# A graph attention edge pass: ScalarE's exponentials before its copy of a block, TensorE's first block behind the turn of the maxima

## What is computed

```python
src, dst = (edge_index[0], edge_index[1])
xl = (x @ W_l + b_l).reshape(n, HEADS, C)
xr = (x @ W_r + b_r).reshape(n, HEADS, C)
e = (edge_attr @ W_e).reshape(-1, HEADS, C)
g = jax.nn.leaky_relu(xl[src] + xr[dst] + e, NEG_SLOPE)
logits = jnp.einsum('ehc,hc->eh', g, att)
amax = jax.ops.segment_max(logits, dst, num_segments=n)
ex = jnp.exp(logits - amax[dst])
denom = jax.ops.segment_sum(ex, dst, num_segments=n)
alpha = ex / (denom[dst] + 1e-16)
out = jax.ops.segment_sum(xl[src] * alpha[..., None], dst, num_segments=n)
```

## Time and profile before

| What | Value |
|---|---|
| median of 3 timed runs | 5762.61 us |
| range of the timed runs | 5761.96 to 5765.02 us |
| span of the profiled execution, the only time known of it | 6618.7 us |
| span over median | 856.1 us, 14.9% |
| TensorE busy | 4926.0 us (74%) |
| VectorE busy | 3854.6 us (58%) |
| ScalarE busy | 1920.7 us (29%) |
| GpSimd busy | 4014.0 us (61%) |
| mean granted TensorE clock | 0.630 of full speed |

### The profile page before, as it was taken

How to read it: one execution, slowest core, us unless ns; L and a number is a source line. 1 busy time by engine, 2 the same in 40 slices (tenths; PEclk the granted TensorE clock), 3 DMA queues, 4 the chain that set the end, 5 groups by cost and what they waited for, 6 DMA issues and landing times. The chain is left out here.

```text
span 6618.7 us, 104783 instructions
## 1 busy us (share of the span) xinstructions
PE 4926.0 (74%) x33518; PEld 3702.2 (56%) x33518; DVE 3854.6 (58%) x7688; ACT 1920.7 (29%) x4445; POOL 4014.0 (61%) x4125
## 2 busy tenths in 40 slices
PE   5566777777777776467777777777776469999689
PEld 4455666766667765356666566666655332222289
DVE  3122355555555542356666666666665469999855
ACT  1111222222222211112222222222211149999811
POOL 4555566666666665366666666666666627787634
PEclk6555566565565555555555555555555579999899
DMA  6644355555555544244444444444444334343298
GB/s 164 113 111 132 103 150 150 148 144 146 145 149 149 148 136 116 65 118 130 132 132 131 131 127 130 132 131 131 131 131 115 72 101 129 124 129 124 69 336 301
DMA packets 897045, 902.75 MB, mean 136 GB/s; under 512 B 635824, under 2 KB 779480, under 8 KB 880373
## 3 DMA queue, kind: packets, MB, share of 16 engines
q1 hardware_dynamic: 568404, 708.29, 33.9%
q0 software_dynamic: 115488, 115.45, 9.0%
q10 hardware_dynamic: 212608, 72.31, 4.8%
HBM read 656.88 MB, written 239.54 MB: 135 GB/s over the span
## 5 line engine op out<-in xcount | busy, mean ns | idle before, releaser
L507 POOL DMA_INDIRECT mlp_G<-mlp_src,src_cols x1612 | 1531.3, 950 | 1027.5 <-PE mlp_z L873 480.7
L507 POOL DMA_INDIRECT gatv_G<-gatv_src,src_cols x1612 | 1529.2, 949 | 940.1 <-DMA X<-in_x 435.7
L691 DVE TENSOR_TENSOR mlp_hots<-mlp_in_psum,src_lo 128x1024 bf16<-128x1024 bf16 x608 | 416.6, 685 | 734.3 <-remote 573.7
L909 PE MATMUL gatv_sums<-gatv_msg,gatv_same 128*128 128x68 f32 x3234 | 712.0, 390 | 151.7 <-issue 149.8
L909 PEld LDWEIGHTS gatv_sums<-gatv_msg,gatv_same 128*128 128x128 f32 x3234 | 688.2, 310 | 171.2 <-issue 169.1
L909 PE MATMUL mlp_sums<-mlp_zs,mlp_same 128*128 128x64 f32 x3234 | 676.5, 389 | 64.8 <-issue 64.6
L909 PEld LDWEIGHTS mlp_sums<-mlp_zs,mlp_same 128*128 128x128 f32 x3234 | 648.4, 301 | 66.0 <-issue 65.9
L2201 POOL TENSOR_TENSOR keys<-src_lo,gsoft_ring 128x512 f32<-128x512 f32 (+1 forms) x448 | 505.1, 1133 | 182.5 <-ACT src_lo L2344 172.7
L2266 PE MATMUL gsoft_acc<-keys,masks 128*64 128x512 f32 (+1 forms) x1568 | 558.2, 621 | 77.0 <-DVE keys L2440 42.1
L869 PE MATMUL gatv_z<-attr_w,gatv_attrT 112*128 112x448 f32 x462 | 422.3, 1017 | 206.3 <-DVE gatv_msg L597 107.9
L873 PE MATMUL mlp_z<-mlp_win,mlp_hot 128*128 128x64 bf16 x4851 | 384.6, 232 | 240.2 <-issue 236.2
(11 more groups left out here) (481 smaller groups left out, 8498.5 us busy)
## 6 DMA issues: line engine op xcount, KB each, us to landing
mean_block<-blocks SPq DMA_DIRECT2D x62, 1568.0 KB
gsoft_ring<-blocks SPq DMA_DIRECT2D x105, 896.0 KB
sums_gatv<-gatv_out_rows SPq DMA_DIRECT2D x231, 252.0 KB
mlp_rel<-rel_rows SPq DMA_DIRECT2D x116, 448.0 KB
gatv_rel<-rel_rows SPq DMA_DIRECT2D x116, 448.0 KB
sums_mlp<-mlp_out_rows SPq DMA_DIRECT2D x231, 224.0 KB
blocks<-masks SPq DMA_DIRECT2D x31, 1568.0 KB
blocks<-work SPq DMA_DIRECT2D x31, 1568.0 KB
```

The lines of the kernel that those rows point to most:

```text
L507: pool.indirect_dma_start(out=G[:, b.gq, j * L.gathered:(j + 1) * L.gathered], out_offset=None, in_=L.gather_table, in_offset=bass.Indirec ...
L691: last = nc.vector.tensor_tensor(hot_of[:, slot(b, k), :, :, :], bc(steps2_of[:, 0:w, :], 1, [P, OCTET // K2, w, K2]), bc(of_step[:, cols] ...
L909: last = pe.matmul(sums[b.q % 2][:, j * L.msg:(j + 1) * L.msg], same[:, b.q, j, :], rhs, start=True, stop=True)
```

## The change

In the second pass ScalarE's copy of block 1 of batch d moves from ahead of `exponentiate(d)` to behind `nonlinear(i)`. TensorE's block 0 of batch p moves from ahead of `make_z(i+1)` to between `turn_max(p)` and `turn_logits(i)`. The first pass keeps its order. No instruction is added or removed, and no wait condition is changed.

```diff
@@ ScalarE, step(i) @@
                 p, d = i + (-1), i + (-2)
-                if d.exists() and builds(d):
+                if not soft and d.exists() and builds(d):
                     copy_octet(d, per_batch - 1)
                 if soft and d.exists():
                     exponentiate(d)
                 if L.window and i.exists():
                     nonlinear(i)
+                if soft and d.exists() and builds(d):
+                    copy_octet(d, per_batch - 1)
                 if p.exists() and builds(p):
                     copy_octet(p, 0)
@@ TensorE, step(i) @@
                 p = i + (-1)
-                if p.exists() and builds(p):
+                if not soft and p.exists() and builds(p):
                     build_octet(p, 0)
                 if L.window and (i + 1).exists():
                     make_z(i + 1)
@@
                 if soft and p.exists():
                     turn_max(p)
+                    if builds(p):
+                        build_octet(p, 0)
                 if soft and i.exists():
                     turn_logits(i)
```

## The result

The kernel after the change takes **5720.11 us** (median of 4, 5718.07 to 5721.94); the kernel before took 5763.82 us beside it (4 runs, 5761.96 to 5771.25). The ratio is 0.9918, 95% interval 0.9904 to 0.9932: faster by 0.8%, 44 us. The forecast was 5655 us, a gain of 108. Direction and range held. The gain forecast was two and a half times too large.

The account below looks back on a forecast made before the run. The ring was taken to bound batches with blocks: 9.31 - 1.69 + 0.81 = 8.43 us, below GpSimd's 8.75, so 0.56 us times 192 is 108 us gained. 5762.6 - 108 = 5655 us, range 5585 to 5780.

Parts of the forecast that it names:

- The floor: GpSimd's gathers, second pass: seven a batch cost 8.75 us, the next bound once the ring is shorter.
- The ring's 9.31 us: Batches with blocks: cycle of last block, copy, exponentials, weighing, `gatv_z`, turns, sums; 9.31 us, taken as the bound.
- ScalarE's 1.69 us out of the ring: Copy, exponentials, weighing and handover leave the cycle, covered by TensorE's sums and last block: 1.69 us less a batch.
- The sign that I gave for it: In the changed kernel's profile, exponentials (L774) start within 0.3 us of L590's end; before, 2.5 us.
- The first block's 0.81 in the chain: TensorE's first block, formerly built during a wait, now stands between two turns and adds 0.81 us a batch.
- The upper bound of the gain: TensorE's own work as floor, if GpSimd is shorter in timed runs: 0.88 us a batch, 169 us.
- The 0.73 us from the block's recorded end to its copy: TensorE to ScalarE: by the skill's rule 0.73 us belongs to the ring, making the gain 1.29 us a batch, 248 us.
- Rival 1: GpSimd's gather train binds the timed runs too: 0 to 25 us gained, 5738 to 5763; chance 0.20.
- Rival 2: VectorE's weighing is held by adding the gathered rows, not by ScalarE: no gain, 5763 us; chance 0.11.
- Rival 3: Slower: behind late gathers TensorE's first block adds 0.81 us a batch, 39 to 156 us in all; chance 0.14.
- Rival 4: More than forecast: the ring loses 0.73 us too, or TensorE's clock rises: up to 357 us, 5406; chance 0.08.

Follow-up runs that it names:

- ScalarE's part alone: Kernel before with only ScalarE's copy of block 1 moved behind the ReLU, TensorE's order as before: 5804.42 us, ratio 1.0061.
- the pair that lifts the floor: Kernel before and kernel after, each with one gather in seven left out in the second pass from its ninth batch: 5703.59 and 5539.98 us.
- before again: Kernel before, unchanged, profiled a second time: 5749.23 us, span 5747.5 us, 9.00 us a batch with blocks.

## Why the prediction was right in direction and wrong in size

**The floor: right.** GpSimd's "8.75, which becomes the next bound" measured 8.77, and the kernel after, 180 us faster with six gathers, shows it to be that bound.

**The ring's 9.31 us: the step that failed.** The mechanism held, but this term of "9.31 - 8.75 = 0.56 us a batch" was sized too large. In the ordinary execution a batch takes 9.00, not 9.31, so the gain is 0.23 us and not 0.56; times 192 that is 44 us for 108. Of the 0.31 us, 0.21 are the turn at 1.2 GHz itself (9.10 in the timeline above): it is the sums, 3.14 reckoned and 2.89 measured. The 3.14 was read in a long execution, where the sums stood still once and were longer than the 0.33 us of that accounts for; what stretched them is open. The other 0.10 are what two things leave together, neither of which the sum had: 44 of 166 batches are at 2.4 GHz and take 8.12 us, and the 122 others take 9.33 on average, some of them behind late gathers. That the balance is as small as 0.10 is chance, and the executions' own spread is as large. The granted clock of the stretch is 0.59, in the execution that was read 0.53. A gain that is the small difference of two large terms was thus taken from an execution in which both terms were known to be off, and only one of them (GpSimd's 10.28) was set aside for that.

**ScalarE's 1.69 us out of the ring: right in kind.** The weighing waits 33.2 us instead of 185.6. The sign that I gave for it (L774 within 0.3 us of L590's end) didn't come: 4008.48 is 1.08 behind 4007.40. The middle value of the 171 batches of 2400 to 3900 is 1.08 too, and 29 are within 0.3. ScalarE is then issuing the window transfers (4006.95, 1.41 us), which the prediction placed "ahead of both places" and priced at nothing. It was right to, as the cover of TensorE's 4 us took them too. The sign would have been a poor one: in ScalarE's part alone, which is slower, L774 follows within 0.3 us in all 163 batches.

**The first block's 0.81 in the chain: right.** It stands behind L886 as said, and TensorE's own work, 8.43 reckoned, is 8.11 in the row, and 8.11 on average with six gathers where the clock is at 1.2 GHz. The upper bound of the gain, 169 us, came out at 164 in the pair that lifts the floor. That they agree so well is luck: 8.98 less 7.98 in the two profiled executions would be 192 us, and both terms of the 0.88 were too large.

**The 0.73 us from the block's recorded end to its copy.** In the ordinary execution the copy starts 0.03 us behind the recorded end, and so it does within 0.01 us in all 167 copies of 2400 to 3900 that ScalarE stood waiting for over 3 us. In the long execution the same distance is anything from 0.04 to 6.4 us. The 248 us that the sum would give by the rule of the Trainium skill (Perfetto Trace Analysis, "Per-engine timelines") were therefore not there. The rule that TensorE's end is computed isn't refuted by it; a delay read once was no part of the ring.

**The rivals.** Rival 1, the gather train binding, is what one sees in the executions of 6700 us: 6706 against 6700. At 5765 it came true only halfway, since the train was 0.23 us under the ring.

Rival 2 fell: the late gathers bind after the change, but not before. The sign given for it came all the same, as the gather's waits (262.6 us) are now more than ScalarE's were (185.6); it fits a kernel that has met the gathers as well as one that never left them, and the time that moved tells the two apart.

Rival 3's mechanism, a block in the chain behind a late gather, is real. By its rows it is what made ScalarE's part alone slower by 35 us, though no run isolates it; TensorE's new order takes it away, since the block there stands behind `gatv_z`. Its sign can't tell anything: the sums start 1.91 us before L590 in before again (3308.23, 3310.14) and 1.28 after (4005.95, 4007.23), but the block now between the turns moves them by itself.

Rival 4's clock showed itself (0.59 before, 0.64 after) and could bring nothing under the gathers. It is also a rival for the 44 us: with 82 of 170 batches at the higher level, as after, the old durations (8.12 and 9.33) would average 8.75 as well. The levels apart rule it out, as the clock alone would leave both as they were: at 1.2 GHz a batch fell from 9.33 to 8.58 us, and at the higher level it rose from 8.12 to 8.99, as it must where the gathers set the pace. The row given for the clock's direction bears little: in the first pass that the prediction calls denser, TensorE is busy 77% of the stretch, in the second 78%.

## What to carry to other kernels

When the profiled execution is much longer than the timed ones, take a second profile before reading a small difference from it. With one profile only, put the error of each term (here 0.3 of 9.3 us) against the gain (0.56) and widen the forecast to its lower side. Ask of each sign named beforehand whether a rival would give it too. A ring and a floor next to it are told apart by lightening the floor: one gather in seven less moved the kernel before by 65 us and the kernel after by 180. Two moves that look additive can be worthless singly, when each leaves a wait that the other removes.

## What was not expected of the hardware

The same program takes two times, by job: 5764 to 5769 us in three jobs, 6701 and 6700 in two others, each steady within 0.6%. Both jobs of 6700 us ran on one chip, and the two experiments' jobs of 5769 and 5768 us on two others, so it may go by the chip; no run tries that. The profiled execution shown ahead of the prediction (6618.7) is like the second kind (10.41 us a batch, and four window loads of SyncE that take 6.75 us to issue), although its timed runs are of the first. The rows differ not in the durations of the engines' own instructions (the sums take 3.09 us in both) but in what lies between them. This is the timeline of the kernel after in the job of 6700 us; "remote" means that nothing in the profile is seen to end the wait.

```profile
4000.21 5.86 SPq L170 DMA_DIRECT2D gatv_win<-gatv_dst  x4
...
4004.36 0.39 PE L886 MATMUL gatv_z<-ident,gatv_segmax 28*128 28x28 f32 x1 [0.47 <-issue]
...
4005.86 0.50 ACT L789 ACTIVATE masks<-gatv_build_ps 128x392 bf16<-128x392 f32 x1 [5.71 <-remote]
4005.86 0.69 DVE L691 TENSOR_TENSOR gatv_hots<-gatv_in_psum,src_lo 128x1024 bf16<-128x1024 bf16 x1 [1.19 <-remote]
4006.31 0.95 POOL L507 DMA_INDIRECT gatv_G<-gatv_src,src_cols  x1 [2.17 <-DMA X<-in_x]
```

SyncE's four window loads take 5.86 us to issue there, and 1.90 in the ordinary execution at about the same time (from 4001.28). ScalarE and VectorE go on at the same instant, 4005.86, and GpSimd has lost 2.17 us before its next gather, once in a batch: 10.55 us a batch (995 gathers in 3400 to 4900) for 8.77. What stalls them together stays open; no run was made on it. This is why an execution of this kind can't price the ring of the other.
